# Moving half of a feed-forward stage between two pairs of projection tiles

## What is computed

```
latent = x @ basis_w.T                                   # rank 64
lt     = einsum('btr,hrs->bhts', latent, head_mats)      # one 64x64 matrix a head
att    = softmax(causal(lt @ latent.T / 8))
y      = (att @ (x @ v_w.T + v_b)) @ o_w.T + o_b
x      = layernorm(x + y)                                # LN1
h      = gelu(x @ sign(w1).T * alpha1 + b1)              # 1024 -> 4096
x      = layernorm(x + h @ sign(w2).T * alpha2 + b2)     # 4096 -> 1024, LN2
```

## Time and profile before

| what | value |
|---|---|
| median of 5 runs | 3645.91 us (3634.28 to 3703.66) |
| the five runs | 3645.91, 3639.45, 3703.66, 3652.42, 3634.28 us |
| the profiled execution | 3645.91 us |
| its span on the slowest core (core 3) | 3644.1 us |
| spans of the other cores | 3609.4 to 3640.1 us |
| mean granted TensorE clock, die 0 and die 1 | 0.780 and 0.781 |

### The profile page before, as it was taken

One profiled execution on the slowest core, in us unless ns is written; L12 is line 12 of the kernel. 1 busy time (PEld: TensorE's weight loads), 2 busy tenths in 40 slices (PEclk: granted clock), 3 DMA queues, 4 the chain that ended last, 5 costly groups with the idle time before them and its releaser, 6 DMA issues.

```text
span 3644.1 us, 37035 instructions; the slowest of 8 cores (3609.4 to 3644.1 us)
## 1 busy us (share of the span) xinstructions
PE 2217.7 (61%) x12698; PEld 1208.4 (33%) x12698; DVE 1220.4 (33%) x2058; ACT 1135.8 (31%) x1647; POOL 92.5 (3%) x158
## 2 busy tenths in 40 slices
PE   1211376857667477675756567665667577675665
PEld 0000143424343243432434243433334243432443
DVE  2465515242324403234152424243242422333100
ACT  0233033512445036450213024321335125461210
POOL 1111000000000000000000000000000000000000
PEclk9555687878788788887868787887878787887877
DMA  6899132322232131311323222321322211212233
GB/s 131 238 273 256 51 94 73 92 78 59 73 95 67 44 94 47 90 48 60 88 70 96 84 57 84 96 78 58 76 75 79 73 53 59 86 59 70 72 109 108
DMA packets 331550, 327.27 MB, mean 90 GB/s; under 512 B 16621, under 2 KB 304365, under 8 KB 331370
## 3 DMA queue, kind: packets, MB, share of 16 engines
q1 hardware_dynamic: 302362, 303.80, 27.5%
q0 software_dynamic: 29008, 21.11, 4.0%
HBM read 310.96 MB, written 25.17 MB: 92 GB/s over the span
## 4 chain that ended last, share of the span: by engine, by line
PE 44%; DMA 22%; DVE 15%; ACT 10%; issue 7%; POOL 1%; DVEq 0%; SPq 0%; ACTq 0%; POOLq 0%
PE pF L977 12%; PE pSX L922 9%; DMA sw2b<-sw2scr 9%; DMA sw1b<-sw1scr 6%; ACT Pp L696 5%; PE pO L713 4%; PE pSW L805 4%; DMA sw2scr<-x2T 3%; PE pSW L655 3%; PE pO L583 3%; PE pO L718 3%; DMA sw1scr<-x2T 3%; DVE bnsc L777 2%; DVE lrec L725 2%; PE pSX L655 2%
## 5 line engine op out<-in xcount | busy, mean ns | idle before, releaser
L977 PE MATMUL pF<-hbuf,sw2b 128*128 128x256 bf16 x4096 | 641.0, 311 | 211.0 <-DMA sw2b<-sw2scr 203.7
L922 PE MATMUL pSX<-x2T,sw1b 128*128 128x256 bf16 x4096 | 511.3, 283 | 155.7 <-DMA sw1b<-sw1scr 137.3
L977 PEld LDWEIGHTS pF<-hbuf,sw2b 128*128 128x128 fp8e4 x4096 | 432.4, 110 | 419.3 <-issue 304.8
L922 PEld LDWEIGHTS pSX<-x2T,sw1b 128*128 128x128 fp8e4 x4096 | 386.1, 100 | 281.2 <-issue 213.9
L669 DVE SCALAR_TENSOR_TENSOR pSW<-pSW,masks 128x512 f32<-128x512 f32 (+1 forms) x128 | 72.4, 566 | 910.0 <-PE pSW L660 910.0
L938 ACT ACTIVATE hbuf<-pSX,b1c_s,al1c 128x256 bf16<-128x256 f32 x512 | 288.7, 567 | 256.7 <-PE pSX L922 256.4
L696 ACT ACTIVATE Pp<-pSW,negmc 128x1024 bf16<-128x1024 f32 x256 | 285.5, 1115 | 207.2 <-DVE pSW L675 89.8
L655 PE MATMUL pSW<-qp,latd 64*128 64x512 bf16 x320 | 139.8, 437 | 318.0 <-ACT Pp L696 166.9
L713 PE MATMUL pO<-Pp,Vt 128*65 128x512 bf16 (+3 forms) x640 | 270.4, 423 | 84.2 <-ACT Pp L703 82.3
L718 PE MATMUL pO<-Pp,Vt 128*65 128x512 bf16 (+3 forms) x640 | 258.3, 404 | 0.0
L938 ACT ACT_TABLE_LOAD x15 | 19.2, 1283 | 715.6 <-PE pSX L922 715.6
(11 more groups left out here) (108 smaller groups left out, 2167.1 us busy)
## 6 DMA issues: line engine op xcount, KB each, us to landing
sw2b<-sw2scr SPq DMA_DIRECT2D x512, 256.0 KB, 2.7
sw1b<-sw1scr SPq DMA_DIRECT2D x128, 512.0 KB, 4.1
xres<-hs SPq DMA_DIRECT2D x32, 512.0 KB, 4.0
out<-outb SPq DMA_DIRECT2D x32, 512.0 KB, 2.7
xT<-hsT POOLq DMA_DIRECT2D x16, 512.0 KB, 7.3
hbuf<-w1n SPq DMA_DIRECT2D x16, 512.0 KB, 9.3
hbuf<-w1t SPq DMA_DIRECT2D x16, 512.0 KB, 10.2
y2t<-w1t SPq DMA_DIRECT2D x16, 512.0 KB, 9.8
```

Of the source, the lines that this page charges most:

```text
L922: bank=bank, toff=toff: e.matmul(bank[:, 0:HF], sw1b[par][:, k, 128 * cl:128 * cl + 128], x2T[:, k, toff:toff + HF], start=(k == 0), stop= ...
L977: stp=stp: e.matmul(bank[:, boff:boff + HF], sw2b[par][:, hcl, 128 * dc:128 * dc + 128], hbuf[:, hc, :], start=stt, stop=stp),
```

## The change

`emit_oproj_ln1` takes a range of tiles. The main loop emits tiles 0 and 1, then `ffn_stage(0)`, then tiles 2 and 3. A new pair of counts, `x2T_half`, records VectorE's count after the copies of tile 1 and of tile 3, and `gen_ffn1` waits for the one of its half in place of `x2T_ready`.

```
--- before.py
+++ after.py
@@ -244,6 +244,7 @@
         "sw2_load": [0, 0], "sw2_free": [0, 0],
         "pp_free": [0, 0],
         "negm_ready": 0, "x2_ready": 0, "x2T_ready": 0, "h_done": 0,
+        "x2T_half": [0, 0],
     }
     pre = {'sw1_blk': {}, 'sw2_blk': {}, 'al1_ready': {}}
     wn_free = [0, 0, 0, 0]
@@ -794,8 +795,8 @@
                 waits=([("pool", pw)] if i == 0 else []), inc="dve")
         return P.c("dve")
 
-    def emit_oproj_ln1(s, ci):
-        for tt in range(TT):
+    def emit_oproj_ln1(s, ci, tiles=None):
+        for tt in (range(TT) if tiles is None else tiles):
             par = tt % 2
             for coh in range(c.NH):
                 dstp = pS if coh % 2 == 0 else pS2
@@ -857,6 +858,7 @@
                 setg(gname, "dve", P.c("dve"))
                 x2t_evac[0] = P.c("dve")
             x2b_free[0] = P.c("pe")
+            st_["x2T_half"][min(1, tt // c.HT)] = P.c("dve")
         st_["x2_ready"] = P.c("dve")
         st_["x2T_ready"] = P.c("dve")
 
@@ -925,7 +927,7 @@
                                  x2T[:, k, toff:toff + HF],
                                  start=(k == 0), stop=(k == CC - 1)),
                              waits=([(f"g_sw1{par}", st_["sw1_load"][par]),
-                                     ("dve", st_["x2T_ready"]),
+                                     ("dve", st_["x2T_half"][half]),
                                      ("act", h_free[co % 2])] + guard(gname)
                                     if k == 0 else []),
                              inc="pe" if k == CC - 1 else None)
@@ -1145,10 +1147,10 @@
             for g in list(fills):
                 drain_all(g)
             if more():
-                emit_oproj_ln1(s, ci)
-            if phase[0] <= TRUNC:
+                emit_oproj_ln1(s, ci, range(0, c.HT))
                 prev_chunk = (s, ci)
                 ffn_stage(0)
+                emit_oproj_ln1(s, ci, range(c.HT, TT))
     for g in list(fills):
         drain_all(g)
     ffn_stage(1)
```

## The result

The changed kernel takes 3655.53 us (median of 40 runs, 3640.91 to 3756.31) against 3639.45 for the kernel before (77 runs). The ratio is 1.0047 with a 95% interval of 1.0032 to 1.0062: slower by 0.47%, some 17 us. With this many runs that is clear of no change, and its sign is not the forecast's: -3.8 us was forecast. The time itself lies inside the stated range of 3625 to 3662, but only because that range is wide on the slow side. Some executions of both kernels had one die at a lower clock; the ratio leaves them out.

What follows compares the result with a forecast made beforehand. No single engine was the limit: a sequence of stages with different limits, TensorE busy 61% of the span. Terms -18.8 + 14.0 + 1 = -3.8 us took 3645.9 to 3642, range 3625 to 3662.

Steps and rivals of the forecast that it cites:

- No wait is covered: Transposes of every tile: all 32 layer-norm waits keep their 7.77 us or more, 0 change.
- The exchange between x2T's copies: Feed-forward half's wait of about 0.5 us on x2T moves behind tile 1, tile 3's follower needs none: 0.
- The close call in chunk 0: First weight load, not prefetched, stays hidden by about 1.4 us: 0; otherwise at most some 5.7 us once.
- The rival of covered layer norms: Feed-forward half covers layer norms of tiles 2 and 3: 16 waits vanish, -124 us, 3522; chance 0.02.
- the one of a free latent stage: Tile 2 keeps its clock gain and the latent stage pays nothing: -18.8 us, 3627; chance 0.07.
- The gain: Tile 2's projection behind the feed-forward half runs at the upper clock: 2.35 us a chunk, -18.8 us in eight.
- The clock at the latent stage: First latent stage behind tile 3 starts at the 1.2 GHz level: +2.0 us in seven chunks, +14.0; bounds 0 and +20.0.
- The sign that the prediction had named for a loss of this kind: Profile sign of a wrong forecast: 32-matmul groups of L583 in the latent stages over 10 us.
- The second yardstick: Cold start read from the other three projection tiles, 5.10, 5.40 and 5.30 us: 1.73 us over 3.54.
- The rival with a wholly cold latent stage: Latent stage stays at the 1.2 GHz level: 6.34 us a chunk, +26.6 us net, 3672; chance 0.06.
- The last chunk's own term: Second feed-forward stage: 0.81 us wait goes, first 16 matmuls start at the lower clock: +1, bounds -0.8 and +1.9.
- equal cold starts: Skill rule's count of cold starts per chunk, five before and five after: sum of 0 and 3646 us.

Runs made afterwards that it cites:

- the interleaved kernel: Changed kernel with 7 of the feed-forward half's 32 groups in tile 2's layer-norm wait, 8 in tile 3's, 17 behind tile 3: 3479.64 us, 0.9562 against the kernel before.
- one moved tile: Changed kernel with only tile 3 behind the feed-forward half, tiles 0 to 2 ahead of it: ratio 1.0004 (0.9979 to 1.0028) to the kernel before.

## Why the prediction was wrong

**What held.** No wait is covered (297.1 us before the transposes, L924 on x2T and on weights as before), and the reason given for it was the right one: the interleaved kernel differs by where the groups stand in TensorE's program, and gained what the prediction priced for 16 covered waits. The exchange between x2T's copies held. The close call in chunk 0 stayed hidden: the feed-forward half there starts 0.47 us behind x2T's last copy and waits for no weights. The rival of covered layer norms and the one of a free latent stage are refuted by the change's own profile.

**The gain was right.** Tile 2 was to gain 2.35 us and gained 2.34 on the mean of the cores, 5.90 to 3.56, and 2.27 on the slowest core, 5.89 to 3.62; times 8, -18.7 against -18.8.

**The step that failed: "The clock at the latent stage", with its value of +2.0 us a chunk and its bound of +2.85.** Its mechanism was right, its size was not. It measured +0.86 for the first group, as predicted, +2.46 for the V group against the 0.55 to 1.99 that I had allowed, and +0.1 for the small matmul: +3.4 a chunk, +24 us in seven in place of +14.0. This is outside the bound and alone it turns the sign: 24 - 14 = +10 us on a forecast of -3.8. I had taken the nearest rows from second latent stages. Those stand behind feed-forward steps that keep TensorE in part busy, and three of their seven V groups were at 7.08 even in the changed kernel. Behind a tile no V group was under 9.28 us on the slowest core. The sign that the prediction had named for a loss of this kind, V groups over 10 us, did not show; the longest there took 9.74. The second yardstick, a projection tile's cold start of 1.73 us, was too low, probably for another reason: its 16 matmuls run in one piece, while the latent stage is a short group, a wait of 1.1 to 1.5 us for the square, and then the long group. The run with 34 extra matmuls points that way, since there the first group behind the transposes kept the clock and the V group behind the wait did not; no run took the wait out of the cold latent stage. The rival with a wholly cold latent stage (+6.34) had the right sign and nearly twice the size.

**Terms left out.** Tile 3 got slower, 5.18 to 5.65 us (+0.47, +3.8 us in eight) and tile 1 by 0.2 (+1.8); the second latent stage with its steps got 0.4 us longer (V-2nd 7.43 to 8.04, and its steps 0.2 shorter), +2.7. The prediction put all three at nothing, without a reason. In every run where tile 2 is fast and tile 3 stands behind its layer norm, tile 3 takes 5.44 to 5.68 us, against 5.09 and 5.18 in the order of before; why it does, and why V-2nd differs from run to run (7.37 to 8.10), no run isolates. All of them together: -18.7 + 24 + 3.8 + 1.8 + 2.7 = +13.6, and the attention stages add 2.2; read directly, the seams, attention and the last chunk give 14.4. The last chunk's own term, +1, is small: on the slowest core the wait of 0.81 us went to 0.48 and the first 16 matmuls on sw2b from 1.91 to 3.57, as the prediction had it. Of these 1.3 us 0.8 are hidden by a shorter wait for the next weights. Over the whole last chunk nothing of it is left: it is 2.3 us shorter, as much as the gain of its tile 2.

**What made it cold.** The prediction spoke of a wait and transposes in one breath. The runs take them apart. Wait filled with 28 matmuls, then 1.72 us idle and the transposes: clock lost. Filled with 34: the first group kept it, the V group behind its wait did not. Filled through the transposes: all of the latent stage kept it, save where the level of 0.81 came in. And behind feed-forward groups that reach to the transposes (interleaved run) the next projection kept it. The rule of the Trainium skill that I had weighed (TensorE: Matmul & The Clock Gate, "HAM oscillation — how this bites in real kernels": dense work should stand together) agrees with this case in its direction. Counted as equal cold starts it gave 3646 and a sum of 0. A cold start here cost 1.5 to 2.3 us for a tile (5.09 to 5.90 against 3.56) and 3.4 for the latent stage, so the count was no measure of it.

What stays open is what made tile 3 and the second latent stage slower, and whether one moved tile costs less than two; the time of that run can't tell. The traces also leave open how much of the latent stage's 3.4 us goes back to the wait in its middle.

## What to carry to other kernels

An engine that runs its program in order covers a wait only with work that stands between the two instructions around the wait; moving a block to the other side of such a pair moves the wait and nothing else. Before a dense stage is moved, look at what will stand behind each thin stretch afterwards: the clock penalty is paid by the next work, and here it was larger for a short group with a wait behind it (3.4 us) than for one long group (1.5 to 2.3 us). Take the price for such a place from rows with the same work ahead of them, and where there are none, widen the bound past the worst row.

## What the runs showed of the hardware

Transposes as such, eight of 128 columns in some 2.6 us with VectorE's copies between, did not lower the granted clock when dense matmuls reached up to them: the projection behind them took 3.6 us. With 1.72 us of idle time ahead of them they did, and the group behind them took 1.92 us in place of 1.06. With dense matmuls up to them and a short group with a wait of 1.49 us behind them, the group took 1.06 us and the V group behind the wait 8.49 in place of 7.08.

Matmuls whose result nobody reads, put into a wait that exists anyway, bought time with no change to the computation. How much depended on how far they reached: with 28 in tile 3's wait the changed kernel still stood at 1.0025, with 34 at 0.9984, with 34 and one more behind each transpose at 0.9955; 28 in all four waits of the kernel before gave 0.9951 (each ratio against the kernel before on the same chip). In the two runs with 34, and in no other, the granted clock stood in short stretches at 0.81 on two neighbouring cores at a time, and a V group under it took 8.57 us. The interleaved kernel, which fills the waits of tiles 2 and 3 with work that is needed, gained far more (0.9562) and shows none of it.
